# A graph layer on one Trainium2 core: TensorE's order of the two subtractions of v's parts, the next block's G and the second sums

## The chip, the core and the metric

The kernel runs on one core of a Trainium2 chip. Its engines are TensorE (PE in the profile; its weight loads are shown apart as PEld), VectorE (DVE), ScalarE (ACT), GpSimd (POOL) and SyncE (SP). Each engine works through its own list of instructions in the order in which they were written, and stops at a wait until a semaphore has the value asked for. The metric is the device time of one execution in microseconds, the median of three runs; less is better.

## The reference

For each of 53,125 edges the features of both end nodes are taken, two small tensor-product layers are applied whose weights come from a per-edge two-layer network (`_mlp`), the result is scaled and summed over the edges that arrive at each of 3,125 nodes, added to x and normalised over 32 channels.

```
r = edge_vec / norm(edge_vec);  sh1 = sqrt(3) * r
s1 = concat([x[src][:, :8], x[dst][:, :8]])             # (E, 16)
v1 = concat([x[src][:, 8:], x[dst][:, 8:]])             # (E, 16, 3)
w  = relu(emb @ fc1_w1 / sqrt(10)) @ fc1_w2 / 4         # (E, 512) -> Wss, Wvv, Wsv, Wvs
s_t = a1 * (s1 . Wss + (v1 . sh1 / sqrt(3)) . Wvv)
v_t = a1 * ((s1 . Wsv) * sh1 + v1 . Wvs)                # first layer, 8 + 8x3 per edge
w2 = relu(emb @ fc2_w1 / sqrt(10)) @ fc2_w2 / 4         # (E, 384)
scal, gates, vecs = second layer on s_t, v_t with w2    # same form
edge_out = concat([tanh(scal), vecs * tanh(gates)]) * norm
return layernorm(x + segment_sum(edge_out, dst))
```

## The kernel before

**Tiling.** The edges, sorted by destination, are cut into NB = 104 blocks of BE = 512 edges (T = 4 tiles of 128). Most arrays hold features or hidden units on the 128 partitions and the 512 edges of a block along the free dimension. PSUM is one tensor `ps` of eight banks of 128x512 fp32.

**The path of a block m.** Source rows come by indirect DMA into `xs`, destination rows by a one-hot product (`spread_places`, `spread_edges`, `rows`); ACT and POOL build `fe`; `turn_features` transposes it, ACT copies it to `f`. Then
- `first_layer(m)` (L1073), which the change's name calls **G**: four fp32 products into banks 0 to 3. It waits for `f_copied` and for `z_done`, m - 1 times: banks 0 to 3 are shared with `repeat`, so DVE must have read the repeated v of block m - 2 out of them. Its semaphore is `g_done`.
- `products(m)` on DVE (L751): banks 0 to 3 times the hidden layer `h1`, to `p_s`.
- `sum_1(m)` (L986): four fp32 products that sum `p_s` to `v_ps` in bank 7.
- v is turned into three bf16 parts by ACT and TensorE in turns. `part_of_v(m, 0)` (ACT, L528) copies bank 7 to `v_s` as bf16; `less_part(m, 0)` (PE, L993), the **first subtraction**, takes that part off in bank 7; `part_of_v(m, 1)` copies the rest; `less_part(m, 1)`, the **second subtraction**, takes it off; `part_of_v(m, 2)` copies what is left. Each step waits for the one before (semaphores `s1_step` and `v_step`).
- `repeat(m)` (L1029): four bf16 products that spread v over banks 0 to 3, once all three parts are there and `products(m + 1)` has read the banks; `products2(m)` on DVE (L791): times `h2`, to `z_s`; its semaphore is `z_done`.
- `sum_2(m)` (L1004), the **second sums**: four fp32 products into bank 5; ACT copies them to `u` (L500).
- `turn(m)` (L1053): four transposes of `u` into bank 7, the same bank in which v of a later block is parted. It therefore waits until the third copy of v is done. DVE reads bank 7 in `gates(m)` (L802, L805, L807), and the tanh, the weights, the outputs and the sums over nodes (`over_nodes`, L1021) follow.

The wait in `turn(k)` and the order of the loops are what the change's steps touch:

```
bank = 0 if k == NB - 1 else 7
if k < NB - 1:
    pe.wait_ge(v_step, 3 * min(k + 3, NB))
```

With k = i - 2 this asks, in step i, for all three copies of block i's v.

**The order.** A software pipeline over `STEPS`, i from -5 to NB; in step i each engine does pieces of several blocks, in an order written out by hand. TensorE's step i begins with `repeat(i - 1)`, `hidden_2(i)` (L1066), `sum_1(i)`, `over_nodes(i - 5)`, `spread_edges(i + 4)` (L964), `rows(i + 3)` (L1041), `hidden_1(i + 1)` (L1060), and ends with `turn(i - 2)` and `turn_features(i + 2)` (L974). ACT's step i is `hidden_2`, `part_of_v(i, 0)`, `hidden_1` (L534), `part_of_v(i, 1)`, `copy_rows` (L513), `copy_sources` (L506), `copy_one_hot` (L523), `copy_oht` (L488, it waits for `spread_places`, L948), `part_of_v(i, 2)`, `tanhs` (L482), `copy_u` (L500), `copy_f` (L494). DVE's step i is `products(i)`, `gates(i - 3)`, `products2(i - 1)` and then small pieces, the last of them `sum_along(i + 2)` (L785).

Of the kernel before, what the change touches and what calls it, by code (L numbers as in the profile page):

```python
# [47 lines left out]
def program(nc, xp, xt, src_t, dst_t, dst_rows, base_col, bases_row, emb, vec_t, wgt, w1, w2a, w2b, out):  # L48
    ctx = ExitStack()
    with ctx:  # L50
# [216 lines left out]
        def real(m):  # L267
            return 0 <= m < NB
# [666 lines left out]
        def _(pe):  # L935
            def spread_places(m):

                pe.wait_ge(place_loaded[(m // CB) % 3], 16 * (m // (3 * CB) + 1))
                if m == 0:
                    pe.wait_ge(spread_ready, 1)  # L940
                if m >= 1:
                    pe.wait_ge(oht_copied, m)
                if m >= 4:
                    pe.wait_ge(h2_ready, m - 3)
                if m >= 9:
                    pe.wait_ge(acc_done, m - 8)
                first = m % CB * BE
                nc.tensor.matmul(oht_ps, spread[:].rearrange("p m n -> p (m n)"), place_r[(m // CB) % 3][:, first:first + BE],  # L948
                                 start=True, stop=True).then_inc(oht_spread, 1)

            def spread_edges(m):

                pe.wait_ge(place_loaded[(m // CB) % 3], 16 * (m // (3 * CB) + 1))
                if m == 0:
                    pe.wait_ge(spread_ready, 1)
                if m >= 1:
                    pe.wait_ge(ohs_ready, m)
                if m >= 2:
                    pe.wait_ge(rows_copied, m - 1)
                if m >= 3:  # L960
                    pe.wait_ge(f_copied, m - 2)
                first = m % CB * BE
                for t in range(T):
                    last = nc.tensor.matmul(ohs_ps[:, t, :], place_r[(m // CB) % 3][:, first + TE * t:first + TE * t + TE],  # L964
                                            spread[:, :, 0], start=True, stop=True)
                last.then_inc(ohs_spread, 1)
# [11 lines left out]
            def sum_1(m):  # L978
                pe.wait_ge(p_done, m + 1)
                if m == 0:  # L980
                    pe.wait_ge(consts_ready, 1)
                    pe.wait_ge(rep_step, 6)
                if m >= 3:
                    pe.wait_ge(e_free, m - 2)
                for g in range(4):
                    last = nc.tensor.matmul(v_ps[32 * g:32 * g + 32], sum_m[:].rearrange("p n c -> p (n c)"), p_s[:, g, :],  # L986
                                            start=True, stop=True)
                last.then_inc(s1_step, 1)

            def less_part(m, n):  # L990

                pe.wait_ge(v_step, 3 * m + n + 1)
                nc.tensor.matmul(v_ps, less[n][:], v_s[:], start=False, stop=True, skip_group_check=True).then_inc(s1_step, 1)  # L993

            def sum_2(k):
                pe.wait_ge(z_done, k + 1)
                if k == 0:
                    pe.wait_ge(weights_ready, 4)
                    pe.wait_ge(consts_ready, 3)
                pe.wait_ge(h1_ready, min(k + 3, NB))  # L1000
                if k + 2 >= NB:
                    pe.wait_ge(u_ready, k)
                for g in range(4):
                    last = nc.tensor.matmul(s2_ps[32 * g:32 * g + 32], w_z[:, min(g, 1), :], z_s[:, g, :],  # L1004
                                            start=True, stop=True)
                last.then_inc(s2_done, 1)

            def over_nodes(k):
                pe.wait_ge(eo_done, k + 1)
                if k == NB - 3:  # L1010
                    pe.wait_ge(f_copied, NB)
                elif k == NB - 2:
                    pe.wait_ge(u_ready, NB)
                elif k == NB - 1:
                    pe.wait_ge(acc_done, NB - 3)
                elif k + 6 > NB:
                    pe.wait_ge(acc_done, k)
                pe.wait_ge(h2_ready, min(k + 6, NB))
                bank = node_bank.get(k, 6)
                for t in range(T):  # L1020
                    last = nc.tensor.matmul(ps[32 * t:32 * t + 32, bank, 0:WIN], eo_all[:, k, t, 8:OC], ohs_r[k % OH][:, t, :],  # L1021
                                            start=True, stop=True)
                last.then_inc(node_done, 1)

            def repeat(k):
                pe.wait_ge(p_done, min(k + 2, NB))
                pe.wait_ge(v_step, 3 * k + 3)
                for g in range(4):
                    last = nc.tensor.matmul(ps[:, g, :], rep_m[32 * g:32 * g + 32, g].rearrange("p j c -> p (j c)"), v_s[32 * g:32 * g + 32],  # L1029
                                            start=True, stop=True)  # L1030
                last.then_inc(rep_done, 1)
# [24 lines left out]
            def hidden_1(m):  # L1056
                pe.wait_ge(emb_loaded[m % 3], 48 * (m // 3 + 1))
                if m >= 3:
                    pe.wait_ge(u_ready, m - 2)
                nc.tensor.matmul(h1_ps, w_first[:, 0, :], emb_r[m % 3][:], start=True, stop=True).then_inc(h1_done, 1)  # L1060

            def hidden_2(m):
                pe.wait_ge(oht_copied, min(m + 4, NB))
                if m + 3 >= NB:
                    pe.wait_ge(acc_done, m - 5)
                nc.tensor.matmul(h2_ps, w_first[:, 1, :], emb_r[m % 3][:], start=True, stop=True).then_inc(h2_done, 1)  # L1066

            def first_layer(m):
                pe.wait_ge(f_copied, m + 1)
                if m >= 2:  # L1070
                    pe.wait_ge(z_done, m - 1)
                for g in range(4):
                    last = nc.tensor.matmul(ps[:, g, :], w_f[32 * g:32 * g + 32], f_r[m % 2][32 * g:32 * g + 32],  # L1073
                                            start=True, stop=True)
                last.then_inc(g_done, 1)

            def misfits_of_all():
                pe.wait_ge(pool_consts, 5)
                pe.wait_ge(misfit_parts, 1)
                nc.tensor.matmul(ps[0:1, 7, 0:1], ext[0:NB], ones[0:NB], start=True, stop=True).then_inc(misfit_sum, 1)  # L1080

            def keep_warm(n):
                for _ in range(n):
                    nc.tensor.matmul(ps[:, 1, 0:128], ident[:], ident[:], start=True, stop=True)
# [8 lines left out]
            for i in STEPS:  # L1093
                if i == -4:
                    pe.wait_ge(pool_consts, 5)
                    keep_warm(12)
                    misfits_of_all()
                    pe.wait_ge(misfits_ready, 1)
                    flag = pe.value_load(misfits[0:1, 0:1], min_val=0, max_val=EP)
                    spread_places(0)  # L1100
                if real(i - 1):
                    repeat(i - 1)
                if real(i):
                    hidden_2(i)
                if real(i):
                    sum_1(i)
                if real(i - 5):
                    over_nodes(i - 5)
                if real(i + 4):
                    spread_edges(i + 4)  # L1110
                if real(i + 3):
                    rows(i + 3)
                if i == -1:
                    pe.wait_ge(weights_ready, 3)
                    pe.wait_ge(misfits_ready, 1)
                if real(i + 1):
                    hidden_1(i + 1)
                if real(i):
                    less_part(i, 0)
                if real(i + 1):  # L1120
                    first_layer(i + 1)
                if real(i + 4) and i + 4 >= 1:
                    spread_places(i + 4)
                if real(i):
                    less_part(i, 1)
                if i == NB:
                    turn(i - 2)
                if real(i - 1):
                    sum_2(i - 1)
                if real(i - 2) and i < NB:  # L1130
                    turn(i - 2)
                if real(i + 2):
                    turn_features(i + 2)
# [82 lines left out]
```

## Time and profile before

| | us |
|---|---|
| median of 3 runs (746.05 to 746.92) | 746.08 |
| the profiled execution's own time | 744.64 |
| its span, from the first to the last instruction | 742.8 |
| PE busy (with the modelled ends of its matmuls) | 687.2 (93%) |
| DVE busy | 691.7 (93%) |
| ACT busy | 560.2 (75%) |
| POOL busy | 528.0 (71%) |

The profiled execution took 744.64 us, 1.44 us less than the median; 1.84 us of it lie outside the span. The span has a start of about 50 us, in which constants, places and embeddings are prepared, and then the 104 steps. In the rows below a time is microseconds from the span's start.

### The profile page before, as it was taken

To read this page: it belongs to the slowest core of one execution; us is meant where nothing else is said; L and a number is where in the kernel's file an instruction comes from. 1 tells how busy PE (TensorE), PEld (TensorE's weight loads), DVE (VectorE), ACT (ScalarE), POOL (GpSimd) and SP (SyncE) were. 2 spreads that over 40 slices of the span, in tenths; PEclk is the share of its full clock that TensorE was granted. 3 is DMA by queue.
4 is the path that set the end of the run, shared out by engine and by line. 5 is a ranking of instruction groups with operands and counts; after the bars stand their busy time and mean duration, and the time that the engine had idled before them with its cause. 6 is when DMAs were issued, how large, how long until landed. Compare 5 with 4: busy or idle time off the path is not lost.

```text
span 742.8 us, 19328 instructions
## 1 busy us (share of the span) xinstructions
PE 687.2 (93%) x5990; PEld 282.9 (38%) x5990; DVE 691.7 (93%) x1231; ACT 560.2 (75%) x1281; POOL 528.0 (71%) x653
## 2 busy tenths in 40 slices
PE   2359999999999999999999999999999999999984
PEld 2113334434443444344344444334434443444321
DVE  7488999999999999999999999999999999999986
ACT  3238887887888778888888888877788888878752
POOL 5676888778876887688768886787778876887200
PEclk7569999999999999999999999999999999999998
DMA  5412211111111211121112111211121111111000
GB/s 132 112 34 47 47 32 28 40 46 28 30 42 27 50 26 42 28 47 31 43 26 45 29 43 27 48 31 27 40 46 29 28 39 26 41 27 27 20 1 23
DMA packets 45822, 28.49 MB, mean 38 GB/s; under 512 B 23299, under 2 KB 43941, under 8 KB 45721
## 3 DMA queue, kind: packets, MB, share of 16 engines
q1 hardware_dynamic: 31402, 19.43, 9.9%
q0 software_dynamic: 13312, 6.84, 6.0%
q8 instruction: 52, 0.85, 0.5%
q10 hardware_dynamic: 1006, 0.96, 0.5%
q14 instruction: 50, 0.40, 0.2%
HBM read 22.46 MB, written 4.74 MB: 37 GB/s over the span
## 4 chain that ended last, share of the span: by engine, by line
PE 87%; DVE 4%; issue 2%; ACT 1%; POOL 1%; DVEq 0%; ACTq 0%
PE ps L1073 16%; PE ps L986 14%; PE ps L1004 13%; PE ps L993 9%; PE ps L1053 8%; PE ps L974 6%; PE ps L1029 5%; PE ps L1066 4%; PE ps L1060 3%; PE ps L964 3%; PE ps L1041 3%; PE ps L948 2%; PE ps L1021 2%; DVE p_s L751 2%; ACT v_s L528 1%
## 5 line engine op out<-in xcount | busy, mean ns | idle before, releaser
L374 POOL DMA_INDIRECT xs<-in_xp,src_i x416 | 401.0, 964 | 115.2 <-issue 104.3
L751 DVE TENSOR_TENSOR p_s<-ps,h 128x2048 f32<-128x2048 f32 x104 | 238.3, 2292 | 21.6 <-PE ps L1073 20.9
L791 DVE TENSOR_TENSOR z_s<-ps,h 128x2048 f32<-128x2048 f32 x104 | 237.6, 2284 | 1.3 <-PE ps L1029 1.2
L528 ACT CAST v_s<-ps 128x512 bf16<-128x512 f32 x312 | 182.2, 584 | 48.3 <-PE ps L986 43.2
L1073 PE MATMUL ps<-f,w_f 32*128 32x512 f32 x832 | 119.7, 642 | 4.3
L986 PE MATMUL ps<-p_s,sum_m 128*32 128x512 f32 x832 | 111.7, 605 | 0.6 <-DVE p_s L751 0.5
L1004 PE MATMUL ps<-z_s,w_z 128*32 128x512 f32 x832 | 110.8, 605 | 1.5 <-DVE z_s L791 1.5
L494 ACT COPY f<-ps 128x512 f32<-128x512 f32 x104 | 61.0, 587 | 41.9 <-PE ps L974 41.5
L993 PE MATMUL ps<-v_s,less 128*128 128x512 bf16 x208 | 81.1, 390 | 2.8 <-ACT v_s L528 2.6
L416 POOL TENSOR_TENSOR along<-fe,r 128x192 f32<-128x192 f32 x104 | 54.2, 521 | 32.8 <-ACT fe L506 26.3
L1053 PEld LDWEIGHTS ps<-ident,u 128*128 128x128 f32 x416 | 43.8, 141 | 87.6 <-issue 87.0
L534 ACT ACTIVATE h<-ps 128x512 f32<-128x512 f32 x104 | 62.2, 598 | 19.7 <-PE ps L1060 12.4
L540 ACT ACTIVATE h<-ps 128x512 f32<-128x512 f32 x104 | 62.2, 598 | 13.7 <-PE ps L1066 8.5
L488 ACT ACTIVATE oht<-ps 126x512 bf16<-126x512 f32 x104 | 62.5, 601 | 11.1 <-POOL e_part L397 5.3
L500 ACT COPY u<-ps 128x512 f32<-128x512 f32 x104 | 61.1, 588 | 12.4 <-PE ps L1004 2.1
L1053 PE MATMUL ps<-ident,u 128*128 128x128 f32 x416 | 68.0, 286 | 1.3 <-DVE m L807 1.0
L974 PE MATMUL ps<-ident,fe 128*128 128x128 f32 x416 | 63.5, 276 | 5.9 <-ACT ohs L523 5.7
L993 PEld LDWEIGHTS ps<-v_s,less 128*128 128x128 bf16 x208 | 19.9, 96 | 89.9 <-ACT v_s L528 78.5
L417 POOL TENSOR_TENSOR fe<-fe,r 128x192 f32<-128x192 f32 x104 | 54.0, 519 | 0.0
L974 PEld LDWEIGHTS ps<-ident,fe 128*128 128x128 f32 x416 | 49.2, 143 | 8.7 <-issue 7.3
L1021 PEld LDWEIGHTS ps<-ohs,eo_all 128*32 128x32 f32 x832 | 25.1, 108 | 68.0 <-issue 65.5
L1073 PEld LDWEIGHTS ps<-f,w_f 32*128 32x128 f32 x832 | 35.3, 185 | 34.2 <-issue 34.2
(129 smaller groups left out, 848.7 us busy)
## 6 DMA issues: line engine op xcount, KB each, us to landing
emb<-e_dram SPq DMA_DIRECT2D x309, 30.0 KB
xs<-in_xp,src_i POOLq DMA_INDIRECT x416
e_dram<-e_part SPq DMA_DIRECT2D x7, 360.0 KB, 3.0
e_in<-in_emb SPq DMA_DIRECT2D x8, 240.0 KB, 2.9
window<-x_dram SPq DMA_DIRECT2D x104, 7.9 KB
eo_all<-in_vec_t SPq DMA_DIRECT2D x1, 528.0 KB, 5.0
x_dram<-eo_all SPq DMA_DIRECT2D x1, 525.0 KB
place<-place_dram SPq DMA_DIRECT2D x26, 20.0 KB
```

Source lines behind the costliest of these rows:

```text
L374: nc.gpsimd.indirect_dma_start(xs_r[n][:, t, :], None, xp, bass.IndirectOffsetOnAxis(src_i[:, m * T + t:m * T + t + 1], axis=0)).then_inc( ...
L488: nc.scalar.activation(oht_r[m % 2][:], oht_ps, ACT.Relu).then_inc(oht_copied, 1)
L528: nc.scalar.copy(v_s[:], v_ps).then_inc(v_step, 1)
L534: nc.scalar.activation(h1_r[m % 2][:], h1_ps, ACT.Relu, scale=1.0 / math.sqrt(10.0)).then_inc(h1_ready, 1)
L751: nc.vector.tensor_tensor(p_s[:], ps[:, 0:4, :], h1_r[m % 2][:].unsqueeze(1).to_broadcast([128, 4, BE]), ALU.mult).then_inc(p_done, 1)
L791: nc.vector.tensor_tensor(z_s[:], ps[:, 0:4, :], h2_r[k % 3][:].unsqueeze(1).to_broadcast([128, 4, BE]), ALU.mult).then_inc(z_done, 1)
L974: last = nc.tensor.transpose(f_ps[:, TE * t:TE * t + TE], fe_r[m % 2][:, t].rearrange("p g c -> p (g c)"), ident[:])
L986: last = nc.tensor.matmul(v_ps[32 * g:32 * g + 32], sum_m[:].rearrange("p n c -> p (n c)"), p_s[:, g, :], start=True, stop=True)
L993: nc.tensor.matmul(v_ps, less[n][:], v_s[:], start=False, stop=True, skip_group_check=True).then_inc(s1_step, 1)
L1004: last = nc.tensor.matmul(s2_ps[32 * g:32 * g + 32], w_z[:, min(g, 1), :], z_s[:, g, :], start=True, stop=True)
L1053: last = nc.tensor.transpose(ps[:, bank, TE * t:TE * t + TE], u_r[k % 2][:, TE * t:TE * t + TE], ident[:])
L1073: last = nc.tensor.matmul(ps[:, g, :], w_f[32 * g:32 * g + 32], f_r[m % 2][32 * g:32 * g + 32], start=True, stop=True)
```

## The change

Within TensorE's step i two calls move; nothing is added or taken away, no wait is altered, and the lists of the other four engines are the same. `less_part(i, 0)` stands behind `first_layer(i + 1)` in place of ahead of it, and `less_part(i, 1)` behind `sum_2(i - 1)` in place of ahead of it.

```
                 if real(i + 1):
                     hidden_1(i + 1)
+                if real(i + 1):
+                    first_layer(i + 1)
                 if real(i):
                     less_part(i, 0)
-                if real(i + 1):
-                    first_layer(i + 1)
                 if real(i + 4) and i + 4 >= 1:
                     spread_places(i + 4)
-                if real(i):
-                    less_part(i, 1)
                 if i == NB:
                     turn(i - 2)
                 if real(i - 1):
                     sum_2(i - 1)
+                if real(i):
+                    less_part(i, 1)
                 if real(i - 2) and i < NB:
                     turn(i - 2)
```

TensorE's list in one step in the middle of the kernel before, from `hidden_1` (L1060) to `turn_features` (L974). `ps` is the PSUM tensor, each row gives line, output and inputs:

```order
506 L1060 MATMUL ps<-emb,w_first 128x512
507 L993 MATMUL ps<-v_s,less 128x512
508 L1073 MATMUL ps<-f,w_f 128x512 x4
509 L948 MATMUL ps<-place,spread 126x512
510 L993 MATMUL ps<-v_s,less 128x512
511 L1004 MATMUL ps<-z_s,w_z 32x512 x4
512 L1053 MATMUL ps<-ident,u 128x128 x4
513 L974 MATMUL ps<-ident,fe 128x128 x4
```

The same step of TensorE in the changed kernel:

```order
506 L1060 MATMUL ps<-emb,w_first 128x512
507 L1073 MATMUL ps<-f,w_f 128x512 x4
508 L993 MATMUL ps<-v_s,less 128x512
509 L948 MATMUL ps<-place,spread 126x512
510 L1004 MATMUL ps<-z_s,w_z 32x512 x4
511 L993 MATMUL ps<-v_s,less 128x512
512 L1053 MATMUL ps<-ident,u 128x128 x4
513 L974 MATMUL ps<-ident,fe 128x128 x4
```

The first L993 now follows G (L1073), and the second stands directly ahead of the transposes of L1053, with the second sums (L1004) ahead of it.

## Rows read from the trace of the kernel before

**Rows 1.** The page, its first part: busy us, share of span, instructions.
```profile
PE 687.2 (93%) x5990; PEld 282.9 (38%) x5990; DVE 691.7 (93%) x1231; ACT 560.2 (75%) x1281; POOL 528.0 (71%) x653
```

**Rows 2.** Busy time by stretch: the steady part, then one step of it.
```profile
core 0: us, PE busy (x) PEld busy (x) DVE busy (x) ACT busy (x) POOL busy (x), PEclk, DMA share, GB/s
60.00:725.00 665.00, 654.49 (x5757) 268.00 (x5753) 638.13 (x1113) 533.51 (x1224) 488.07 (x603) 1.00 0.16 34
405.49:411.98 6.49, 6.44 (x58) 2.69 (x57) 6.31 (x12) 5.12 (x13) 5.37 (x8) 1.00 0.13 26
```

**Rows 3.** Timeline from `products2` on: start us, us, engine, line, out<-in; idle before.
```profile
405.49 2.28 DVE L791 TENSOR_TENSOR z_s<-ps,h 128x2048 f32<-128x2048 f32 x1
...
407.48 0.39 PE L993 MATMUL ps<-v_s,less 128*128 128x512 bf16 x1
...
407.89 0.34 PEld L1073 LDWEIGHTS ps<-f,w_f 32*128 32x128 f32 x8 [0.32 <-issue]
407.92 1.14 PE L1073 MATMUL ps<-f,w_f 32*128 32x512 f32 x8
...
408.85 0.38 PE L948 MATMUL ps<-place,spread 5*126 5x512 bf16 x1
...
409.12 2.29 DVE L751 TENSOR_TENSOR p_s<-ps,h 128x2048 f32<-128x2048 f32 x1
```

**Rows 4.** Waits of the whole span: who waited for whom, us, times, longest.
```profile
PEld ps L993 <- ACT v_s L528: 78.5, 174, 1.0
...
DVE p_s L751 <- PE ps L1073: 20.9, 97, 1.1
```

**Rows 5.** Timeline, TensorE and DVE in the rest of that step.
```profile
409.16 0.10 PEld L993 LDWEIGHTS ps<-v_s,less 128*128 128x128 bf16 x1 [0.60 <-ACT v_s L528]
409.16 0.39 PE L993 MATMUL ps<-v_s,less 128*128 128x512 bf16 x1
...
409.48 1.07 PE L1004 MATMUL ps<-z_s,w_z 128*32 128x512 f32 x8
...
410.48 0.65 PE L1053 MATMUL ps<-ident,u 128*128 128x128 f32 x4
...
410.97 0.60 PE L974 MATMUL ps<-ident,fe 128*128 128x128 f32 x4
411.32 0.25 DVE L802 TENSOR_TENSOR m<-ps,r 128x96 f32<-128x96 f32 x1
...
411.50 0.10 PEld L1029 LDWEIGHTS ps<-v_s,rep_m 32*128 32x128 bf16 x4 [0.17 <-DVE p_s L751]
411.50 0.39 PE L1029 MATMUL ps<-v_s,rep_m 32*128 32x512 bf16 x4
...
411.98 2.29 DVE L791 TENSOR_TENSOR z_s<-ps,h 128x2048 f32<-128x2048 f32 x1
```

**Rows 6.** Timeline, ScalarE between the three copies of v in that step.
```profile
406.84 0.59 ACT L528 CAST v_s<-ps 128x512 bf16<-128x512 f32 x1 [0.48 <-PE ps L986]
...
408.25 0.58 ACT L528 CAST v_s<-ps 128x512 bf16<-128x512 f32 x1
...
408.71 0.28 ACT L513 COPY fe<-ps 128x128 f32<-128x128 f32 x1
...
409.07 0.33 ACT L523 ACTIVATE ohs<-ps 128x168 f32<-128x168 f32 x1
...
409.27 0.62 ACT L488 ACTIVATE oht<-ps 126x512 bf16<-126x512 f32 x1
...
409.76 0.61 ACT L528 CAST v_s<-ps 128x512 bf16<-128x512 f32 x1
```

**Rows 7.** The chain of waits, in order of time, its piece of `turn_features`.
```profile
411.13 0.44 PE ps L974 x4
```

**Rows 8.** Timeline near 53 us, where TensorE's granted clock was 0.50.
```profile
52.83 1.94 PE L986 MATMUL ps<-p_s,sum_m 128*32 128x512 f32 x8
```

**Rows 9.** Busy time by stretch, that stretch, columns as in rows 2.
```profile
50.00:55.00 5.00, 3.26 (x19) 0.67 (x20) 4.28 (x4) 0.77 (x2) 3.78 (x5) 0.50 0.10 17
```

More of the change, by code:

```diff
@@ L1117, in _ @@
                     hidden_1(i + 1)
+                if real(i + 1):
+                    first_layer(i + 1)
                 if real(i):
                     less_part(i, 0)
-                if real(i + 1):
-                    first_layer(i + 1)
                 if real(i + 4) and i + 4 >= 1:
                     spread_places(i + 4)
-                if real(i):
-                    less_part(i, 1)
                 if i == NB:
@@ L1129, in _ @@
                     sum_2(i - 1)
+                if real(i):
+                    less_part(i, 1)
                 if real(i - 2) and i < NB:
```

## Prediction

> **What bounds the kernel now.** I read the page's busy shares first, and they do not name one bound: PE and DVE both stand at 93% [rows 1], and in the steady part both are near full: of the 665 us from 60 to 725 PE is busy for 654 and DVE for 638 [rows 2]. One step takes 6.49 us (from one z_s to the next, 405.49 to 411.98) [rows 3, 5], with DVE busy for 6.31 of it [rows 2]. So the timeline of one step has to say which wait ends last. It shows a loop through both engines. DVE's products2 (z_s) runs from 405.49 to 407.77. G is held until then, since it writes the banks that z_s reads: its weight load starts at 407.89, its products at 407.92, 0.15 after z_s is done; they end at 409.06, and products (p_s) starts at 409.12 [rows 3]. p_s takes 2.29, then gates, and z_s follows at 411.98 [rows 3, 5]. 2.28 + 0.15 + 1.14 + 0.06 (G to p_s) + 2.86 (p_s to z_s, 409.12 to 411.98) = 6.49: the loop closes. DVE's only stop in it is for G, 20.9 us over 97 times, 0.22 a step [rows 4].
>
> TensorE's other side of the step is just as tight: from G's start the second subtraction, sum_2, turn and turn_features follow without a hole, and repeat starts at 411.50, 0.09 after p_s has ended (409.12 + 2.29 = 411.41), with 0.17 idle in the load queue ahead of it [rows 5]. TensorE has thus about 0.1 to spare ahead of repeat, and what is put between G and repeat beyond that is paid for in the length of the step.
>
> **The first subtraction moves behind G.** It removes nothing from G's wait. Today it starts at 407.48 and ends at 407.87; z_s ends at 407.77 and G's load starts at 407.89 [rows 3]. Both could release G. I take z_s, because two other neighbours that follow a 512-column product on TensorE with no wait of their own start after 0.31 (L948 to L993) and 0.32 (L993 to L1004) [rows 3, 5], whereas G's load comes 0.41 after the subtraction's start: something else holds it, and only z_s is left. So G stays at 2.43 us after z_s's start (407.92 - 405.49), and TensorE idles where the subtraction stood. The subtraction's 0.3 now lies behind G, on the path from G to repeat.
>
> **The second subtraction moves behind sum_2.** Its own time only changes places with sum_2's. But v's chain has a third copy behind it, and turn(i - 2) waits for that copy, because both use bank 7. Before, sum_2's 1.00 us (409.48 to 410.48) covered it: the copy started at 409.76 and ended at 410.37, and turn started at 410.48 [rows 5, 6]. Now turn stands directly behind the subtraction, and the copy is bare. In TensorE's queue turn_features and repeat stand behind turn, and for them wait ACT's copy of f, DVE's gates and z_s, and through z_s the next G.
>
> **The sum for a step**, in us after z_s's start:
> 1. G starts at 2.43 [rows 3].
> 2. The first subtraction starts 0.93 later, as spread_places does today (408.85 - 407.92) [rows 3]: 3.36. This product uses all 128 rows of the array where spread_places uses 5, so it may have to wait until the last of G's four is out, at most the whole 1.14: up to 0.21 more. I take 0.93, since the modelled end of sum_2 (409.48 + 1.07 = 410.55) also lies behind the start of the full-array product after it (410.48) [rows 5].
> 3. spread_places and sum_2 follow at the 0.31 and 0.32 of today's neighbours (408.85, 409.16, 409.48) [rows 3, 5]: sum_2 at 3.99, where it is now.
> 4. The second subtraction starts 1.00 later, as turn does today: 4.99.
> 5. Its product takes 0.39 [rows 5], ACT starts 0.03 to 0.07 behind a product's end, the copy takes 0.58 [rows 6], and TensorE picks up 0.05 after it (406.84 + 0.59 = 407.43, subtraction at 407.48) [rows 3, 6]. With 0.03 this is 1.05: turn starts at 6.04, against 4.99 today.
> 6. turn to turn_features 0.49, turn_features to repeat 0.53, repeat to z_s 0.48 (410.48, 410.97, 411.50, 411.98) [rows 5]: the next z_s at 7.54.
>
> A step grows from 6.49 to 7.54, by 1.05. The second move alone brings it; the 0.3 of the first cancels against the second subtraction's leaving the same stretch. Two neighbours could make it more. ACT: the second copy of v now starts at 3.36 + 0.39 + 0.03 = 3.78, and today 1.51 pass from the second copy to the third, four other copies lying between them (408.25 to 409.76) [rows 6]: 5.29, ahead of the 5.41 at which the third copy is released. ACT is no bound, by 0.12. DVE: turn ends at 6.04 + 0.65 = 6.69, gates starts at about 6.75 against 5.83 today (411.32 - 405.49), its three instructions take 0.66 to z_s (411.32 to 411.98) [rows 5]: 7.41, ahead of 7.54. DVE is hidden, by 0.13.
>
> Blocks 2 to 103 have both a subtraction and a turn in their step: 102 steps, 102 x 1.05 = 107 us. Steps 0 and 1 have no turn; their wait for the third copy falls on repeat and I count it at nothing, between 0 and 2 us. The profiled execution took 744.64: 744.64 + 107 = 852; its distance to the median, 1.44, is added: **853 us**.
>
> **The bounds.** Upwards: 0.21 for the first subtraction behind G, 102 x 0.21 = +21. Downwards: turn_features to repeat may be 0.44 and not 0.53 once repeat no longer waits for p_s [rows 7], and repeat to z_s 0.45 (its 0.39 and the 0.06 of G to p_s), 102 x 0.12 = -12. The start may absorb 2 to 3 us of it. That gives 838 to 874, the range.
>
> A rule of the Trainium skill speaks about step 6. The row first: the weight load of the subtractions, whose weights are a constant, sat idle for ACT's copy of v 174 times, 78.5 us [rows 4], so a load did not go ahead of a wait in its own list. "TensorE: Matmul & The Clock Gate", section "Step-by-step: what each phase is for", says that TensorE pulls weight loads ahead of running products. By that, turn's first load would be done under the bare copy, and turn to turn_features would be shorter, by an estimate of some 0.1 us, about 10 us over the kernel; by the row nothing changes, and I go by the row.
>
> **Rivals.**
> - *Only the displaced product counts.* If turn were not held by the third copy (if the semaphore asked for were already there), turn would start an ordinary 0.32 behind the second subtraction, at 5.31, repeat at 6.33 and z_s at 6.81: +0.32 a step, +33, 779 us. Against it: the third copy cannot start before the subtraction's end at 5.38, and the wait is for exactly that copy. 3 in 100, with all between 760 and 838.
> - *G comes earlier.* If it is the first subtraction's end, not z_s's, that releases G today, G moves forward by 0.32 a step. Alone that leaves 7.54 - 0.32 = 7.22, +0.73, 820 us: still slower. 4 in 100.
> - *Faster.* It takes both: G released earlier, and the copy hidden. Then repeat would come at 6.33 - 0.32 = 6.01, the 6.01 of today, DVE would set the pace and lose its stop for G, at most the 20.9 us of rows 4: 725 us. The point from which it decides is where the third copy ends before TensorE reaches turn, 5.31. The copy ends at 5.99, so it is missed by 0.68 us. 2 in 100.
> - *The copy is bare but something slack swallows it (no change).* It would need 1.05 us of idle time a step in the loop; DVE has 0.18 (6.49 - 6.31) [rows 2] and TensorE some 0.1. 1 in 100.
> - *The clock falls.* The idle time of TensorE rises from next to none to about 0.35 ahead of G and 0.7 ahead of turn in 7.54. The granted clock is 1.00 (2.4 GHz) in the whole steady part, with PE almost always busy [rows 2]; it was 0.50 (1.2 GHz) from 50 to 55 us, after a stretch in which TensorE had stood waiting for DVE, and there sum_1's eight records took 1.94 where they take 1.06 at full clock [rows 8, 9]. At that ratio, 1.8, the roughly 4.7 us of TensorE's work in a step's path (7.54 less z_s's 2.28 and the copy's 0.6) would cost 3.8 us more in each slow step; a quarter of the steps at the low level would be +97, some 950 us. The stretches without work here are short and come every step, so I give it 3 in 100. The Trainium skill, same page, section "A second HAM failure mode: psum-queue depth-cycling", describes just such frequent small gaps as making the clock swing; no row of this trace shows it.
> - *ACT is late.* With the third copy more than 0.3 later than by my sum, the time passes 874: 5 in 100.
>
> **Chances.** The forecast, 838 to 874: 82 in 100; the rivals as above: below it 10 (3 + 4 + 2 + 1), above it 8 (3 + 5). A measurement of this kernel tells about 0.2% from no change. Slower by more than that: 0.97; within it: 0.01; faster: 0.02.
>
> **What will show it.** If right: z_s to z_s near 7.54 in the steady part; G still 2.43 after z_s's start; turn's load queue idle for ACT's copy of v (L1053 <- L528) some 100 times with 0.6 to 0.8 us each; DVE's gates (L802) waiting for turn about 0.8 us a step and its wait for G (20.9) unchanged, since G is still released by z_s; PE busy well below 93%, clock still 1.00. It is wrong if turn starts at once behind the subtraction, if G starts earlier than 2.43, or if the step has grown by less than 0.9 or more than 1.3 us.

## The result, and the profile after

| | before | after |
|---|---|---|
| median | 746.07 us (745.95 to 746.92, 4 runs) | 872.66 us (871.27 to 874.61, 4 runs) |
| ratio | | 1.170, 95% interval 1.168 to 1.172 |
| span of the profiled execution | 742.8 us | 872.0 us |

The same instructions in another order on one engine cost 17%. The page of the changed kernel, first part, as rows 1:

```profile
PE 715.4 (82%) x5990; PEld 280.0 (32%) x5990; DVE 707.6 (81%) x1231; ACT 562.4 (65%) x1281; POOL 527.5 (60%) x653
```

The counts of instructions are those of rows 1, and each engine is busy for a smaller share of the span. In us, PE and DVE are busy for 28 and 16 more than before. That is not more work for DVE: its 1231 records, each taken by itself, add up to 773 us after and 774 before, but fewer of them overlap where the engine stops more often. For PE, whose ends are modelled, nothing here separates the two. The busy time by stretch, as rows 2 (length, then busy time of each engine, the granted clock, DMA):

```profile
60.00:840.00 780.00, 666.51 (x5710) 260.40 (x5706) 647.57 (x1098) 533.32 (x1217) 488.87 (x603) 1.00 0.14 29
```

One step of the changed kernel in the timeline, against rows 3, 5 and 6:

```profile
402.70 2.29 DVE L791 TENSOR_TENSOR z_s<-ps,h 128x2048 f32<-128x2048 f32 x1
...
405.13 1.14 PE L1073 MATMUL ps<-f,w_f 32*128 32x512 f32 x8 [0.46 <-DVE z_s L791]
...
406.20 0.39 PE L993 MATMUL ps<-v_s,less 128*128 128x512 bf16 x1
...
406.52 0.42 PE L948 MATMUL ps<-place,spread 5*126 5x512 bf16 x1
...
406.63 0.59 ACT L528 CAST v_s<-ps 128x512 bf16<-128x512 f32 x1 [1.32 <-PE ps L993]
...
406.88 1.07 PE L1004 MATMUL ps<-z_s,w_z 128*32 128x512 f32 x8
...
407.88 0.39 PE L993 MATMUL ps<-v_s,less 128*128 128x512 bf16 x1
...
408.30 0.59 ACT L528 CAST v_s<-ps 128x512 bf16<-128x512 f32 x1
...
408.96 0.42 PEld L1053 LDWEIGHTS ps<-ident,u 128*128 128x128 f32 x4 [0.99 <-issue]
408.99 0.63 PE L1053 MATMUL ps<-ident,u 128*128 128x128 f32 x4 [0.72 <-issue]
...
409.45 0.60 PE L974 MATMUL ps<-ident,fe 128*128 128x128 f32 x4
409.65 0.26 DVE L802 TENSOR_TENSOR m<-ps,r 128x96 f32<-128x96 f32 x1 [1.03 <-PE ps L1053]
...
409.99 0.40 PE L1029 MATMUL ps<-v_s,rep_m 32*128 32x512 bf16 x4
...
410.43 2.29 DVE L791 TENSOR_TENSOR z_s<-ps,h 128x2048 f32<-128x2048 f32 x1
```

The step has become 7.73 us (402.70 to 410.43) from 6.49. G still starts 2.43 after z_s, now with TensorE idle for 0.46 ahead of it. The third copy of v ends at 408.89, and turn (L1053) starts at 408.99, after 0.72 of idle time. The waits of the whole span (who waited for whom, us, times, longest) say who pays:

```profile
ACT v_s L528 <- PE ps L993: 132.3, 109, 2.0
DVE m L802 <- PE ps L1053: 105.9, 102, 2.6
...
PE ps L1053 <- issue: 72.9, 101, 0.7
...
DVE p_s L751 <- PE ps L1073: 23.5, 102, 1.6
```

DVE's gates wait for turn, 1.04 us a step in 102 steps, where before they did not; DVE's wait for G (20.9 in rows 4) has stayed. The 72.9 us ahead of turn stand as "issue": turn waits for three semaphores (`u_ready`, `v_step` and `e_free`), and the profile names none for it here. That it is the third copy, the times and the experiment on its length show; the trace of the 32-row run further down names it.

### The profile page after: what moved, and what is told of

Same layout as the page of the kernel before. It is cut to its first block, busy times and chain, and to the rows that moved or that the text cites. A ratio compares the mean times of both kernels' runs of the same rounds, so it can differ in the third digit from the quotient of the medians.

```text
span 872.0 us, 19328 instructions
## 1 busy us (share of the span) xinstructions
PE 715.4 (82%) x5990; PEld 280.0 (32%) x5990; DVE 707.6 (81%) x1231; ACT 562.4 (65%) x1281; POOL 527.5 (60%) x653
## 4 chain that ended last, share of the span: by engine, by line
PE 57%; DVE 25%; issue 12%; ACT 2%; DMA 1%; POOL 1%; DVEq 0%; ACTq 0%; SPq 0%; POOLq 0%
DVE z_s L791 23%; PE ps L1073 14%; PE ps L1004 12%; PE ps L993 8%; PE ps L1053 7%; PE ps L974 5%; PE ps L948 4%; PE ps L1029 4%; ACT e_part L550 1%; ACT h L540 1%; PE ps L1021 1%; POOL xs L374 1%; PE ps L986 1%; DMA src_i<-in_src_t 1%; DVE p_s L751 1%
## 5 line engine op out<-in xcount | busy, mean ns | idle before, releaser
L1073 PE MATMUL ps<-f,w_f 32*128 32x512 f32 x832 | 121.3, 650 | 38.0 <-DVE z_s L791 37.0
L1053 PE MATMUL ps<-ident,u 128*128 128x128 f32 x416 | 65.9, 281 | 74.6 <-issue 72.9
L1004 PE MATMUL ps<-z_s,w_z 128*32 128x512 f32 x832 | 112.5, 613 | 1.5 <-DVE z_s L791 1.5
L802 DVE TENSOR_TENSOR m<-ps,r 128x96 f32<-128x96 f32 x104 | 26.8, 257 | 105.9 <-PE ps L1053 105.9
L993 PE MATMUL ps<-v_s,less 128*128 128x512 bf16 x208 | 81.5, 392 | 0.9 <-ACT v_s L528 0.9
L1053 PEld LDWEIGHTS ps<-ident,u 128*128 128x128 f32 x416 | 44.0, 142 | 103.3 <-issue 102.0
L993 PEld LDWEIGHTS ps<-v_s,less 128*128 128x128 bf16 x208 | 19.9, 96 | 168.0 <-ACT v_s L528 86.9
L974 PE MATMUL ps<-ident,fe 128*128 128x128 f32 x416 | 63.9, 277 | 5.1 <-ACT ohs L523 5.1
L1073 PEld LDWEIGHTS ps<-f,w_f 32*128 32x128 f32 x832 | 36.0, 186 | 66.9 <-issue 66.9
L974 PEld LDWEIGHTS ps<-ident,fe 128*128 128x128 f32 x416 | 49.6, 144 | 7.2 <-issue 7.2
```

The costliest lines, as they stand in the source:

```text
L974: last = nc.tensor.transpose(f_ps[:, TE * t:TE * t + TE], fe_r[m % 2][:, t].rearrange("p g c -> p (g c)"), ident[:])
L1053: last = nc.tensor.transpose(ps[:, bank, TE * t:TE * t + TE], u_r[k % 2][:, TE * t:TE * t + TE], ident[:])
```

## The experiments

**One move at a time.** My prediction said that the second move alone brings the increase, and that the first cancels. The first move alone:

```
-                if real(i):
-                    less_part(i, 0)
                 if real(i + 1):
                     first_layer(i + 1)
+                if real(i):
+                    less_part(i, 0)
```

> The kernel before with the first move alone: the first subtraction behind G, the second where it was, ahead of sum_2. Theory A (the copies of v between ScalarE and TensorE are one chain, and what is put in at its head delays its end): the first subtraction starts at 3.52 us after z_s's start, the second copy at 3.94, then ScalarE's four other copies, the third copy at 5.47 to 6.06, turn at 6.15 in place of 4.99, the next z_s at 7.59. A step of 7.59 us, the whole some 862 us. Theory B (what the prediction said: the second move brings the increase, the first adds only the time of its product, 0.3 us): a step of 6.8 us, 778 us.

Measured: 859.81 us (855.02 to 860.82), ratio 1.150 (1.146 to 1.155). The step is 7.61 us. In its timeline:

```profile
409.43 0.58 ACT L528 CAST v_s<-ps 128x512 bf16<-128x512 f32 x1 [1.32 <-PE ps L993]
...
410.07 0.39 PE L993 MATMUL ps<-v_s,less 128*128 128x512 bf16 x1 [0.32 <-ACT v_s L528]
...
410.47 0.61 ACT L488 ACTIVATE oht<-ps 126x512 bf16<-126x512 f32 x1
410.94 0.61 ACT L528 CAST v_s<-ps 128x512 bf16<-128x512 f32 x1
```

The second subtraction ends at 410.46, but the third copy starts at 410.94, behind copy_oht in ScalarE's list. Theory A stands; theory B, the prediction's own sentence, is out by 82 us.

The second move alone is the other half:

```
-                if real(i):
-                    less_part(i, 1)
                 if real(i - 1):
                     sum_2(i - 1)
+                if real(i):
+                    less_part(i, 1)
```

> The kernel before with the second move alone: the first subtraction ahead of G, the second behind sum_2. Theory A (G still starts at 2.44, sum_2 follows at 3.74, the second subtraction at 4.74, the third copy stands bare ahead of turn at 5.84): a step of 7.29 us, the whole some 831 us. Theory B (the second move alone brings the whole increase): about 870 us. A rival in which the copy is hidden elsewhere: below 760 us.

Measured: 821.1 us (819.96 to 822.6), ratio 1.101 (1.098 to 1.105), a step of 7.23 us. A said 7.29 and 831, B 870. A was out by 0.06 a step, since sum_2 follows spread_places by 0.30 here; that is 6 of the 10 us, and the rest was my addition, since 102 steps of 7.29 give about 828. In its timeline the bare copy stands as in the changed kernel, but 0.5 us earlier in the step (z_s at 400.95):

```profile
405.62 0.39 PE L993 MATMUL ps<-v_s,less 128*128 128x512 bf16 x1
406.05 0.59 ACT L528 CAST v_s<-ps 128x512 bf16<-128x512 f32 x1 [0.72 <-PE ps L993]
...
406.73 0.63 PE L1053 MATMUL ps<-ident,u 128*128 128x128 f32 x4 [0.72 <-issue]
...
408.18 2.29 DVE L791 TENSOR_TENSOR z_s<-ps,h 128x2048 f32<-128x2048 f32 x1
```

The two moves alone cost 114 and 75 us, together 127, not 189. Each delays the end of the third copy, and turn waits for that end only. Turn starts 6.16 us after z_s with the first move alone, 5.79 with the second, 6.29 with both, and 4.99 before.

**ScalarE's list in the first move.** To see whether copy_oht is what made the first move dear by itself, the third copy was put ahead of it, in the kernel first_only:

```
+                if real(i):
+                    part_of_v(i, 2)
                 if real(i + 4) and i + 4 >= 1:
                     copy_oht(i + 4)
-                if real(i):
-                    part_of_v(i, 2)
```

> The kernel first_only (the first move alone, 7.61 us a step), with ScalarE's third copy of v moved ahead of copy_oht. Theory A (in first_only the third copy is released at 4.97 and starts at 5.45 because copy_oht, 0.5 us, stands ahead of it in ScalarE's list): the third copy starts at 5.01, ends at 5.59, turn starts at 5.90 where sum_2 lets it, in place of 6.16: a step of 7.35 us, the whole some 833 us. Theory B (the exchange between TensorE and ScalarE sets the start of the third copy): 7.61 us, 860 us.

Measured: 831.28 us (831.08 to 833.76), a step of 7.37 us; A said 833 and 7.35. The timeline shows copy and turn where A had them (z_s at 398.57):

```profile
403.47 1.06 PE L1004 MATMUL ps<-z_s,w_z 128*32 128x512 f32 x8
403.57 0.59 ACT L528 CAST v_s<-ps 128x512 bf16<-128x512 f32 x1
404.06 0.60 ACT L488 ACTIVATE oht<-ps 126x512 bf16<-126x512 f32 x1
...
404.46 0.66 PE L1053 MATMUL ps<-ident,u 128*128 128x128 f32 x4
```

The copy now hides under sum_2, and turn starts with no idle time, 0.99 after sum_2. What is left, 7.37 against 6.49, is TensorE's own queue: the second subtraction has to wait for the second copy until 4.58 us after z_s, and sum_2 stands behind it.

**The length of the third copy.** In both kernels the third copy was done for half the edges; the other half of the third part of v is left out.

```
-                nc.scalar.copy(v_s[:], v_ps).then_inc(v_step, 1)
+                if n == 2:
+                    nc.scalar.copy(v_s[:, 0:BE // 2], v_ps[:, 0:BE // 2]).then_inc(v_step, 1)
+                else:
+                    nc.scalar.copy(v_s[:], v_ps).then_inc(v_step, 1)
```

> The changed kernel, with the third copy of v done for 256 of its 512 edges only (the other half of the third part is left out). Theory A (the copy's own duration stands bare on the loop): the copy falls from 0.59 to an estimated 0.37 us, worked out from the copies of 128 and 512 elements, and the step by the same 0.2 us: some 851 us. Theory B (what turn waits for is the queue or the semaphores, not the copy's length): 872 us, no change.

> The kernel before, with the third copy of v done for 256 of its 512 edges only (the other half of the third part is left out), the counterpart of half_copy_after, in which a step fell by 0.22 us and the whole by some 24 us. Theory A (before, sum_2 hides the third copy, and turn starts when sum_2 is out): a step stays at 6.49 us, the whole at 746 us, within 2 us. Theory B (a part of the copy was already on the path, or ScalarE was the bound): down to 722 us.

Measured: in the changed kernel 848.32 us (846.46 to 849.78), 24 less than 872.66; in the kernel before 746.27 us (742.84 to 747.79) against 745.93, ratio 1.0005 (0.9987 to 1.0024). The timelines (line numbers are 1 or 3 higher here), first of the changed kernel with half the copy:

```profile
399.40 2.29 DVE L794 TENSOR_TENSOR z_s<-ps,h 128x2048 f32<-128x2048 f32 x1
...
405.02 0.37 ACT L529 CAST v_s<-ps 128x256 bf16<-128x256 f32 x1
...
405.49 0.63 PE L1056 MATMUL ps<-ident,u 128*128 128x128 f32 x4 [0.51 <-issue]
...
406.93 2.29 DVE L794 TENSOR_TENSOR z_s<-ps,h 128x2048 f32<-128x2048 f32 x1
```

and of the kernel before with half the copy:

```profile
398.83 2.28 DVE L794 TENSOR_TENSOR z_s<-ps,h 128x2048 f32<-128x2048 f32 x1
...
403.10 0.37 ACT L529 CAST v_s<-ps 128x256 bf16<-128x256 f32 x1
...
403.82 0.66 PE L1056 MATMUL ps<-ident,u 128*128 128x128 f32 x4
...
405.32 2.28 DVE L794 TENSOR_TENSOR z_s<-ps,h 128x2048 f32<-128x2048 f32 x1
```

The copy is 0.22 to 0.24 shorter. In the changed kernel turn comes 0.2 earlier, 6.09 after z_s, and the step falls to 7.53: the 102 steps from the second z_s to the last take 765.3 us in place of 787.0, 0.21 less each. The rest of the difference lies at the two ends of the kernel. In the kernel before, turn still starts 4.99 after z_s and the step stays 6.49. The copy is bare after, and hidden before.

**Work put into the bare copy's time.** In the changed kernel turn_features was put ahead of turn:

```
+                if real(i + 2):
+                    turn_features(i + 2)
                 if real(i - 2) and i < NB:
                     turn(i - 2)
-                if real(i + 2):
-                    turn_features(i + 2)
```

> The changed kernel with turn_features ahead of turn, so that TensorE works in the bare copy's time. TensorE would reach repeat at 6.84 in place of 7.30 us after z_s's start. Theory A (DVE's gates stands 0.12 us behind as the next bound: they wait for turn, which stays at 6.30): gates at 6.96, z_s at 7.62, a step of 7.62, the whole some 860 us. Theory B (only TensorE's order counts): a step of 7.29, some 826 us.

Measured: 859.72 us (858.67 to 860.75), 13 less, a step of 7.62. In its timeline z_s starts at 402.87. TensorE reaches repeat 0.45 earlier in the step, and DVE uses only 0.12 of it:

```profile
409.71 0.40 PE L1029 MATMUL ps<-v_s,rep_m 32*128 32x512 bf16 x4
409.82 0.26 DVE L802 TENSOR_TENSOR m<-ps,r 128x96 f32<-128x96 f32 x1 [1.03 <-PE ps L1053]
...
410.48 2.28 DVE L791 TENSOR_TENSOR z_s<-ps,h 128x2048 f32<-128x2048 f32 x1
```

repeat is out at 410.11; z_s starts at 410.48, behind gates, which still wait for turn. Theory A stands: the third copy holds turn, and turn is read by DVE directly.

**Why the first subtraction came 1.07 after G.** The prediction had 0.93. In the changed kernel the first subtraction was cut to 32 rows of the array; what it takes off the other 96 rows of v is left out.

```
+                rows = 32 if n == 0 else 128
-                nc.tensor.matmul(v_ps, less[n][:], v_s[:], start=False, ...
+                nc.tensor.matmul(v_ps, less[n][0:rows], v_s[0:rows], start=False, ...
```

> The changed kernel, with the first subtraction as a product over 32 of its 128 rows (what it takes off the other 96 rows of v is left out). Theory A (it started 1.08 us after G's start and not 0.93 because it spans rows of all four of G's products, where spread_places uses the first rows alone): it starts at 3.38 in place of 3.51 us after z_s's start, sum_2 and all behind it 0.1 to 0.14 earlier, a step of 7.6 to 7.64, the whole 858 to 862 us. Theory B (the 1.08 is a handover from an fp32 product to a bf16 one, whatever the rows): 3.51, 872 us.

Measured: 842.28 us (840.15 to 842.81), 30 less, where A had 10 to 14. The timeline, with the weight loads (PEld):

```profile
407.36 1.14 PE L1074 MATMUL ps<-f,w_f 32*128 32x512 f32 x8 [0.43 <-DVE z_s L791]
407.86 0.09 PEld L994 LDWEIGHTS ps<-v_s,less 32*128 32x128 bf16 x1 [0.20 <-issue]
408.29 0.37 PE L994 MATMUL ps<-v_s,less 32*128 32x512 bf16 x1
...
408.51 0.38 PE L948 MATMUL ps<-place,spread 5*126 5x512 bf16 x1
```

A was right on the place: the product starts 0.93 after G, as spread_places does in rows 3, so it is the number of rows that makes the difference. A was wrong on the size, since the cut did more than that: the next product follows after 0.22 in place of 0.32, and sum_2 after 0.30 in place of 0.36. The step fell by 0.28 to about 7.45. Of the product over 32 rows the weight load runs 0.43 ahead, under G; that of the full 128 rows starts with its product (it stood at 406.20 in the changed kernel, and so did its load). Whether the 0.14 comes from the product's own rows or from its earlier load, this run does not separate. About a hundred product records are missing in this trace, and in its waits turn's idle time has a name:

```profile
PE ps L1054 <- ACT v_s L528: 103.8, 99, 1.1
```

L1054 is turn here, and it waits for the copy of v, 99 times. (The 1.05 a time is 0.33 more than the 0.72 above because the second subtraction, whose record is missing, lies in it.)

**The end and the clock.** In the changed kernel the last z_s starts at 849.06, 22.9 us before the span's end; before, 724.24 and 18.6. The stretches of the changed kernel at its end:

```profile
845.00:850.00 5.00, 3.21 (x30) 1.35 (x29) 2.86 (x11) 1.80 (x4) 0.00 (x0) 1.00 0.00 0
850.00:855.00 5.00, 3.61 (x14) 0.66 (x15) 3.26 (x11) 1.00 (x3) 0.00 (x0) 0.54 0.01 2
855.00:860.00 5.00, 5.00 (x49) 1.75 (x49) 2.45 (x12) 1.74 (x3) 0.00 (x0) 0.50 0.02 5
```

The granted clock falls from 1.00 (2.4 GHz) to 0.50 (1.2 GHz), after a stretch in which TensorE was busy for 3.21 of 5 us. Of the last sums this is the price, before and after:

```profile
733.11 1.55 PE L1159 MATMUL ps<-acc,centre 128*32 128x400 f32 x16
```
```profile
860.97 2.90 PE L1159 MATMUL ps<-acc,centre 128*32 128x400 f32 x16
```

Products that nobody reads were then put into the holes of the last steps:

```
+            def warm_end(n):
+                pe.wait_ge(f_copied, NB)
+                for _ in range(n):
+                    nc.tensor.matmul(ps[:, 4, 0:128], ident[:], ident[:], start=True, stop=True)
...
                 if i == NB:
                     turn(i - 2)
+                    warm_end(8)
...
+                if NB - 2 <= i < NB:
+                    warm_end(4)
```

> The changed kernel, with four products that nobody reads ahead of turn in steps 102 and 103 and eight ahead of the last sum_2, in time in which TensorE stood idle. In the changed kernel the granted clock was 0.50 from about 850 us on, and from the last z_s to the end of the span passed 22.95 us against 18.56 before. Theory A (the clock fell because of the larger holes in the last steps, and the work fills them): the clock stays at 1.00 to the last sums, the end takes 18.6 us, the whole some 868 us. Theory B (the end is longer for another reason, or the clock falls all the same): 872 us or a little more.

Measured: 867.45 us (866.66 to 870.43), 5.2 less. Its end by stretch:

```profile
843.00:848.00 5.00, 4.03 (x40) 2.68 (x41) 2.85 (x11) 1.80 (x4) 0.00 (x0) 1.00 0.00 0
848.00:853.00 5.00, 5.00 (x55) 2.57 (x54) 4.05 (x15) 1.00 (x3) 0.00 (x0) 1.00 0.00 2
853.00:858.00 5.00, 3.54 (x44) 1.39 (x40) 2.32 (x11) 1.74 (x3) 0.00 (x0) 1.00 0.02 5
```

The clock stays at 1.00 to the last sums, and the end takes 18.5 us (847.02 to 865.5), as A said. But this does not show A's cause, for two other traces speak against it. In the kernel before with half the third copy neither subtraction was moved; its last z_s starts at 723.80:

```profile
720.00:725.00 5.00, 3.14 (x29) 1.36 (x29) 2.85 (x9) 1.56 (x4) 0.00 (x0) 1.00 0.00 0
725.00:730.00 5.00, 3.86 (x15) 0.91 (x16) 3.00 (x11) 1.00 (x3) 0.00 (x0) 0.57 0.00 2
```

In the changed kernel with half the copy the holes of the changed order are left and nothing fills them; its last z_s starts at 825.99:

```profile
827.00:832.00 5.00, 3.54 (x40) 1.10 (x40) 4.06 (x15) 1.07 (x3) 0.00 (x0) 1.00 0.01 2
```

The first fell to the low level and took 20.2 us from the last z_s to the end; the second kept 1.00 and took 18.6. So the clock can fall at the end without the change and stay up with it, and that the change brings the fall is not shown, nor that the filling prevents it. The two traces also differ in the first step, z_s to z_s: it took 8.21 us with the filling and 10.28 in the changed kernel, though nothing differs there. The clock is at the low level at that point in both, for longer in the changed kernel (0.50 from 57 to 60 us, where it was 1.00 with the filling). What the filling itself is worth of the 5.2 us is therefore open; in these two traces the ends differ by 4.4 and the first steps by 2.1.

## Why the prediction was right, and where it was short

The prediction said 853 us, 838 to 874; measured were 872.66, inside, near the upper end. The loop, the bank that turn shares with v and the bare copy were right. By the steps of its sum, in us, from the timeline of the changed kernel:

| step | forecast | measured |
|---|---|---|
| 1. z_s to G | 2.43 | 2.43 |
| 2. G to the first subtraction | 0.93 | 1.07 |
| 3. to sum_2, by way of spread_places | 0.63 | 0.68 |
| 4. sum_2 to the second subtraction | 1.00 | 1.00 |
| 5. to turn, with the third copy | 1.05 | 1.11 |
| 6. turn to turn_features to repeat to z_s | 0.49, 0.53, 0.48 | 0.46, 0.54, 0.44 |
| a step | 7.54 | 7.73 |

**Step 2 is the term that was mis-sized**, by 0.14. I took the start of a product over five rows for one over all 128, and had named the right bound for it, up to 0.21 more. The 32-row run shows that the number of rows makes the difference. Step 5 was 0.06 short, 0.05 of it because turn starts 0.10 behind the copy's end and not 0.05; step 3 was 0.05 short; step 6 gave 0.06 back. Together 0.19 a step.

**The sum over the kernel.** From the second z_s to the last are 102 steps. They took 664.1 us before and 787.0 after, 1.205 more each: 122.9 in place of 107. (The average is below 7.73 - 6.49 because the kernel before has some steps of 6.5 to 6.8 and the last steps of the changed one are shorter, 7.28 to 7.39.) The other 6.2 us of the 129.1 by which the span grew lie outside them: 4.3 at the end, 2.5 in the first step, less 0.6 ahead of it. I counted no clock there, and both stand in stretches of the low clock. These 6 us are not shown to come from the change (see the end and the clock above), so how near the result came to the upper bound of 874 is in part chance.

**Wrong: "The second move alone brings it; the 0.3 of the first cancels".** Each move alone brings most of it, 114 and 75 us. The sum was made on the whole change only, where TensorE's queue ends just behind ScalarE's; on one move alone I had not followed v's chain through ScalarE's list. There the four other copies, which the prediction itself had counted at 1.51 us, are the longer way.

**The two covers held.** ScalarE was "no bound, by 0.12": the third copy started 0.03 behind the subtraction's end (408.27, 408.30), so TensorE released it. With the 1.51 behind the second copy (406.63) ScalarE would have been ready at 408.14, 0.16 earlier. DVE was "hidden, by 0.13": with turn_features ahead of turn the step fell by 0.12 and no more.

**What would show it.** G at 2.43 and DVE's wait for G unchanged: so. gates waiting about 0.8 us a step: 1.04. turn's wait was to stand against the copy of v, in the load queue; it stands as "issue", 0.72 for the products and 0.99 for the load. PE well below 93%: 82%.

**The rivals.** "Only the displaced product counts" (779), "G comes earlier" (820) and "faster" (725) fell: G did not move, and turn started 0.10 behind the copy's end. So did the one in which something slack swallows the copy. ScalarE was not late either: the third copy came 0.2 later than forecast, all of it from the steps of TensorE ahead of it. The falling clock was a rival for the steps: through 780 us with a hole of 0.46 and one of 0.72 in each step the clock stayed at 1.00. So the swing that the Trainium skill describes ("TensorE: Matmul & The Clock Gate", "A second HAM failure mode: psum-queue depth-cycling") is not in this trace. The first move alone had one short fall near its end: the clock was 0.50 from 822 to 824 us, and the step that began at 816.00 took 8.94 us where the one ahead of it took 7.37.

On turn's weight load the row was right: in the changed kernel the load starts at 408.96, behind the copy's end at 408.89, and a forecast 10 us lower would have been 10 us further off. What the Trainium skill says of weight loads pulled ahead of running products (same page, "Step-by-step: what each phase is for") the 32-row run does show: there the load ran 0.43 ahead of its product, under G's.

## What to carry to other kernels

Where two engines hand one buffer back and forth, the whole chain has to be laid beside the work that covers it, through the lists of both engines. A link moved later costs what its successors then show bare, not its own time, and two such moves need not add up, because only the last link's end counts (114 and 75 us alone, 127 together). Find who waits for that end (here turn, by a shared PSUM bank), and make one run for each part of a change before saying which part costs.

## What the runs showed of the hardware

- A bf16 product over all 128 rows started 1.07 us after G's four fp32 products of 32 rows had begun, one over 5 or 32 rows after 0.93, with its weights loaded 0.42 to 0.43 ahead. After a full one the next 512-column product came 0.32 later, after the 32-row one 0.22.
- The granted clock held 1.00 with TensorE busy for 85.4 of 100 us in regular holes. At the end it fell in the changed kernel after 3.21 busy of 5 us and in the kernel before with half the copy after 3.14 of 5; the kernel before had 3.07 of 5 from 721 to 726 us and the changed one with half the copy 3.15 of 5 from 822 to 827, and both kept 1.00. What decides it stays open.
- The copy of PSUM to bf16 on ScalarE took 0.59 us for 512 elements a partition and 0.37 for 256.
